# A routed two-layer network: rows of a block turned by a transposing DMA, three inner buffers, and the fp16 cast shared by two engines

## The reference

```python
x = x + linear_attention(layernorm(x), W_attn, b_attn, W_proj, b_proj)   # 16 heads of 8
z = layernorm(x)
logits = z @ Wr + br                                # 8 experts
route_w = softmax(logits); top 2, renormalised
h = relu(z @ W1[e] + b1[e])                         # 128 -> 512, for each expert e
expert_out = h @ W2[e] + b2[e]                      # 512 -> 128
x = x + sum over the two chosen e of routed[e] * expert_out[e]
```

## Time and profile before

| | |
|---|---|
| median of 3 runs | 367.26 us (367.24 to 367.77) |
| the profiled execution | 367.57 us |
| its span, first to last instruction | 365.8 us |
| TensorE busy (matmul) | 301.8 us, 83% of the span |
| VectorE busy | 306.2 us, 84% |
| ScalarE busy | 220.0 us, 60% |
| GpSimd busy | 258.0 us, 71% |
| DMA traffic | 29.25 MB, mean 80 GB/s |
| mean granted TensorE clock | 0.935 of full speed |

### The profile page before, as it was taken

The page is one execution under the profiler, slowest core; times in us unless marked ns, Lnnn a source line. Parts: engine busy times, 40 slices in busy tenths (PEclk is TensorE's granted clock), DMA queues, the critical chain, the costliest instruction groups (busy, mean ns, idle before and its releaser), DMA issues.

```text
span 365.8 us, 8190 instructions
## 1 busy us (share of the span) xinstructions
PE 301.8 (83%) x2374; PEld 223.3 (61%) x2377; DVE 306.2 (84%) x622; ACT 220.0 (60%) x644; POOL 258.0 (71%) x254
## 2 busy tenths in 40 slices
PE   5789999779979999899585877999999999998200
PEld 5578755335545445545343766789999999997100
DVE  6988899998787999998897197999888888888186
ACT  2778502387788544444247864667777777775082
POOL 3749999744979999877786663777777777666400
PEclk9999999989999999999786599999999999999755
DMA  7990000000000000011111531224333333211298
GB/s 220 352 282 9 2 0 0 0 4 0 1 0 2 0 15 25 22 37 59 53 44 45 154 82 49 71 68 139 95 88 102 96 97 103 74 43 42 80 391 253
DMA packets 23957, 29.25 MB, mean 80 GB/s; under 512 B 3806, under 2 KB 18569, under 8 KB 23916
## 3 DMA queue, kind: packets, MB, share of 16 engines
q1 hardware_dynamic: 18934, 19.02, 17.9%
q0 software_dynamic: 4544, 9.38, 7.9%
q10 hardware_dynamic: 438, 0.33, 0.3%
HBM read 16.04 MB, written 12.67 MB: 79 GB/s over the span
## 4 chain that ended last, share of the span: by engine, by line
POOL 27%; PE 21%; issue 20%; DVE 19%; ACT 9%; DMA 3%; POOLq 1%; SPq 0%; DVEq 0%; ACTq 0%
POOL y_rows L568 18%; POOL x_rows L528 8%; PE ps L1272 6%; PE ps L1271 4%; DVE nd L926 4%; DVE work L915 3%; PE ps L1245 2%; ACT qk L772 2%; DVE rows L942 2%; ACT v L657 1%; ACT xs L676 1%; DVE x L1206 1%; PE ps L1247 1%; DVE st L801 1%; PE ps L1311 1%
## 5 line engine op out<-in xcount | busy, mean ns | idle before, releaser
L568 POOL DMA_INDIRECT y_rows<-kvt,yid x78 | 74.7, 958 | 29.3 <-issue 19.5
L737 ACT ACTIVATE ps<-ps,b1s 128x256 f32<-128x256 f32 x156 | 60.1, 448 | 35.2 <-PE ps L1427 35.2
L528 POOL DMA_INDIRECT x_rows<-rows,pos_i x64 | 62.4, 975 | 24.5 <-issue 18.0
L1152 DVE CAST wraw<-ps 128x1024 f16<-128x1024 f32 x39 | 47.7, 1224 | 14.0 <-ACT ps L737 11.5
L1156 DVE TENSOR_TENSOR wraw<-ps,wraw 128x1024 f16<-128x1024 f32 x39 | 47.8, 1224 | 1.3
L1425 PE MATMUL ps<-wraw,w1h 128*128 128x256 f16 x156 | 43.4, 278 | 5.7 <-DVE wraw L1156 3.5
L1444 PE MATMUL ps<-w,wraw 128*128 x312 | 45.3, 221 | 0.0
L1445 PE MATMUL ps<-w,wraw 128*128 x312 | 44.9, 221 | 0.0
L1426 PE MATMUL ps<-wraw,w1h 128*128 128x256 f16 x156 | 43.3, 277 | 0.0
L1427 PE MATMUL ps<-wraw,w1l 128*128 128x256 f16 x156 | 43.1, 277 | 0.0
L915 DVE TENSOR_TENSOR work<-ps,qk 128x1024 f32<-128x1024 f32 x32 | 38.0, 1214 | 5.7 <-PE ps L1272 5.6
(11 more groups left out here) (242 smaller groups left out, 768.1 us busy)
## 6 DMA issues: line engine op xcount, KB each, us to landing
wraw<-x_rows SPq DMA_DIRECT2D x39, 130.0 KB
qk<-y_rows SPq DMA_DIRECT2D x8, 512.0 KB, 6.4
wraw<-in_L_ffn_W_dram SPq DMA_DIRECT2D x1, 2048.0 KB, 11.5
out_dram<-x SPq DMA_DIRECT2D x8, 256.0 KB, 4.6
x<-in_L_attn_x_dram SPq DMA_DIRECT2D x3, 512.0 KB, 7.5
y_rows<-kvt,yid POOLq DMA_INDIRECT x78, 2.2
x_rows<-empty SPq DMA_DIRECT2D x9, 130.0 KB, 3.2
x_rows<-rows,pos_i POOLq DMA_INDIRECT x64, 2.4
```

The source lines that it names most:

```text
L528: nc.gpsimd.indirect_dma_start(out=x_rows, out_offset=bass.IndirectOffsetOnAxis(ap=pos_i[:, c, t:t + 1], axis=0), in_=rows[:, t, :], in_of ...
L568: nc.gpsimd.indirect_dma_start(out=y_rows, in_=ysb[:, n % YG, g], in_offset=None, out_offset=bass.IndirectOffsetOnAxis(ap=yid[:, n, g:g + ...
L737: ins = nc.scalar.activation(o, o, ACT.Relu, bias=b1s[:, bass.ds(e * HC + c, 1)])
L1152: nc.vector.tensor_copy(hh[:, n % 2], inner(n)).then_inc(hi_done, 1)
```

## The change

Four things are done together:

- SP's load of a block becomes two. A transposing DMA reads the 256 rows of 256 fp16 numbers from `x_rows` and writes them transposed to `xgT`, which now has six buffers; a second DMA reads the two extra words of each row to `ids`. Both wait for `up_done` of the block six before, in place of `turn_done`. `turn_block` and `copy_turned` are gone, and with them `xg` and PSUM banks 0 and 1 as their place.
- `hh`, `hl` and the PSUM banks of the inner layer are three buffers (`HB`), not two. `up(n)` waits for `lo_done` of block n - 3.
- The cast to `hh` is shared: VectorE casts the first 512 columns, as soon as ScalarE has applied relu to them, and ScalarE the other 512, behind its four relus and a wait for them. `hidden_low` and `down` wait for both.
- The order of rows in a block is different (slot g * 128 + p in place of 2p + g), for `slot_i` and the numbers alike.

Its core:

```diff
+    HB = 3
...
-        hh = in_w(2 * HC * SLOTS, F16).rearrange("p (b c n) -> p b c n", b=2, c=HC)
-        hl = in_w(2 * HC * SLOTS, F16).rearrange("p (b c n) -> p b c n", b=2, c=HC)
-        xg_w = in_w(XG * GPB * ROW).rearrange("p (b n) -> p b n", b=XG)
-        xg = xg_w.rearrange("p b (g w) -> p b g w", g=GPB)
-        xgT = in_w(2 * 2 * SLOTS, F16).rearrange("p (b w n) -> p b w n", b=2, w=2)
+        hh = in_w(HB * HC * SLOTS, F16).rearrange("p (b c n) -> p b c n", b=HB, c=HC)
+        hl = in_w(HB * HC * SLOTS, F16).rearrange("p (b c n) -> p b c n", b=HB, c=HC)
+        xgT = in_w(XG * 2 * SLOTS, F16).rearrange("p (b w n) -> p b w n", b=XG, w=2)
+        ids = in_w(XG * GPB * 2).rearrange("p (b g w) -> p b g w", b=XG, g=GPB)
...
                 if n >= XG:
-                    sp.wait_ge(turn_done, n - XG + 1)
+                    sp.wait_ge(up_done, n - XG + 1)
                     sp.wait_ge(yid_done, n - XG + 1)
-                sp.dma_start(xg_w[:, b, :], x_rows[bass.ds(row, SLOTS), :].rearrange("(p g) w -> p (g w)", g=GPB)
-                             ).then_inc(loaded[b], 16)
+                rows_of_block = x_rows[bass.ds(row, SLOTS), :]
+                sp.dma_start_transpose(xgT[:, b], rows_of_block[:, 0:D].bitcast(F16)).then_inc(x_turned[b], 16)
+                sp.dma_start(ids[:, b], rows_of_block[:, D:ROW].rearrange("(g p) w -> p g w", p=P)).then_inc(ids_in[b], 16)
...
-            def copy_turned(n):
...
                 for c in range(HC):
                     at = c % 2 * SLOTS
-                    o = ps[:, 2 + 2 * (n % 2) + c // 2, at:at + SLOTS]
+                    o = ps[:, 2 * (n % HB) + c // 2, at:at + SLOTS]
                     ins = nc.scalar.activation(o, o, ACT.Relu, bias=b1s[:, bass.ds(e * HC + c, 1)])
-                ins.then_inc(hid_done, 1)
+                    if c % 2 == 1:
+                        ins.then_inc(hid_done, 1)
+                if n >= HB:
+                    act.wait_ge(down_done, n - HB + 1)
+                act.wait_ge(hid_done, 2 * n + 2)
+                nc.scalar.activation(hh[:, n % HB, 2:HC].rearrange("p c n -> p (c n)"), ps[:, 2 * (n % HB) + 1, :],
+                                     ACT.Copy).then_inc(hi2_done, 1)
...
             def hidden_high(n):
-                dve.wait_ge(hid_done, n + 1)
-                if n >= 2:
-                    dve.wait_ge(down_done, n - 1)
-                nc.vector.tensor_copy(hh[:, n % 2], inner(n)).then_inc(hi_done, 1)
+                dve.wait_ge(hid_done, 2 * n + 1)
+                if n >= HB:
+                    dve.wait_ge(down_done, n - HB + 1)
+                nc.vector.tensor_copy(hh[:, n % HB, 0:2], inner(n)[:, 0:2]).then_inc(hi_done, 1)
 
             def hidden_low(n):
                 dve.wait_ge(hi_done, n + 1)
-                nc.vector.tensor_tensor(hl[:, n % 2], inner(n), hh[:, n % 2], ALU.subtract).then_inc(lo_done, 1)
+                dve.wait_ge(hi2_done, n + 1)
+                nc.vector.tensor_tensor(hl[:, n % HB], inner(n), hh[:, n % HB], ALU.subtract).then_inc(lo_done, 1)
...
-            def turn_block(n):
...
-                pe.wait_ge(turn_out, n + 1)
-                if n >= 2:
-                    pe.wait_ge(lo_done, n - 1)
-                xh, xl = xgT[:, n % 2, 0], xgT[:, n % 2, 1]
+                pe.wait_ge(x_turned[n % XG], 16 * (n // XG + 1))
+                if n >= HB:
+                    pe.wait_ge(lo_done, n - HB + 1)
+                xh, xl = xgT[:, n % XG, 0], xgT[:, n % XG, 1]
...
                 pe.wait_ge(hi_done, n + 1)
+                pe.wait_ge(hi2_done, n + 1)
```

More of the change, by code:

```diff
@@ L323, in block_kernel @@
         table_done = sem("table_done")
-        loaded = [sem(f"loaded{b}") for b in range(XG)]
+        x_turned = [sem(f"x_turned{b}") for b in range(XG)]
+        ids_in = [sem(f"ids_in{b}") for b in range(XG)]
         yid_done = sem("yid_done")
-        turn_done = sem("turn_done")
-        turn_out = sem("turn_out")
         up_done = sem("up_done")
@@ L330, in block_kernel @@
         hi_done = sem("hi_done")
+        hi2_done = sem("hi2_done")
         lo_done = sem("lo_done")
@@ L1396, in _ @@
             regs = [pe.alloc_register(name=f"pe_expert{b}") for b in range(4)]
-            def turn_block(n):
-                pe.wait_ge(loaded[n % XG], 16 * (n // XG + 1))
-                if n >= 2:
-                    pe.wait_ge(turn_out, n - 1)
-                both = xg[:, n % XG, :, 0:D].bitcast(F16)
-                for g in range(GPB):
-                    for w in range(2):
-                        at = w * SLOTS + g * P
-                        ins = nc.tensor.matmul(ps[:, n % 2, at:at + P], both[:, g, w * D:(w + 1) * D], ident_h[:, :],
-                                               start=True, stop=True)
-                ins.then_inc(turn_done, 1)
             def up(n):
@@ L1448, in down @@
                     for c in range(HC):
-                        ins = nc.tensor.matmul(o, hl[:, n % 2, c, g * P:(g + 1) * P], high[c], start=False,
+                        ins = nc.tensor.matmul(o, hl[:, n % HB, c, g * P:(g + 1) * P], high[c], start=False,
                                                stop=(g == GPB - 1 and c == HC - 1))
@@ L1465, in _ @@
             logits(U - 1)
-            turn_block(2)
-            turn_block(3)
             for n in range(NBLK):
```

32 lines of the change are left out of this document (9 added, 23 removed).

## The result

The changed kernel takes 363.09 us (median of 4 runs, 362.47 to 364.00) against 367.25 (366.22 to 367.77) for the kernel before on the same chip: a ratio of 0.989, 95% interval 0.986 to 0.992. It is faster by 4.2 us, less than half of the 8.6 that was forecast; the time itself lies inside the stated range, near its upper end. The profiled execution took 364.0, its span 362.3; before it was 367.57 and 365.8.

What follows compares the result with a forecast made beforehand. POOL's row of scatters, started by `pos_i`, was the bound, with TensorE's pace over the last 5.3 us. `pos_i` 0.13 + 2 x 0.55 + 2.04 = 3.27 us earlier and no late waits: 8.6 off 367.57, 359.0; range 356.5 to 363.5.

Steps and rivals of the forecast that it cites:

- What bounds the kernel, `pos_i` first: POOL's scatters start when `pos_i` comes and then hardly rest; `pos_i` was to come 3.27 us earlier, at 220.5.
- Part 1: Before `pos_i`: with three inner buffers TensorE reaches the ranks earlier and VectorE's 2.04 us of idle go.
- Part 2: VectorE's cast shared with ScalarE: 0.69 us in place of 1.23, saving 0.54 to 0.55 a block.
- the handoff: TensorE through ScalarE's relus, half copy and copy of y: 2.88 us, averaged with TensorE's 2.77 to 2.83 a block.
- TensorE's lead: Last copy of y ends at 326.6 us, needed by 332.5: 6 us to spare, so TensorE leaves the end.
- Part 4: Loads on SP's queue: at most 2.6 us a block, latency hidden by a lead of six blocks or 16 us.
- rival A: Transposing DMA on SP's queue and the DMA engines sets the end above 3.2 us a block: about 403 us, 15%.
- Rival C: TensorE keeps 3.10 us a block because the path through ScalarE takes what turning gave: 361.2 us, 7%.
- B: `pos_i` gains less than 3.3 us, as the first transposed block or the clock's rise comes late: 361 us, 16%.
- D: DMA traffic stretches POOL's scatters by 0.1 us each, as much as is gained: 367 us, 3%.
- The sum: POOL's last scatter starts at 333.8, not 342.39, 8.6 us earlier, with 23.4 us behind it unchanged: 359.0 us, 55%.

Runs made afterwards that it cites:

- two banks: Changed kernel with y alternating between two PSUM banks from block 12 on: 359.81 us against 367.28 for the kernel before, ratio 0.980.

## Why the prediction fell short, point by point

- **What bounds the kernel, `pos_i` first**: right. `pos_i` ended at 220.08 (forecast 220.5), POOL took it up 0.77 later and began y at 236.00 (forecast 236.4).
- **Part 1, three inner buffers**: right, the 2.04 us went and the 2.03 stay when the buffers are two.
- **Part 2, the split cast**: the duration was right (0.69; the 1.23 that it starts from is 1.21 in the earlier trace rows, which changes nothing). That ScalarE's half copy would cost the logits nothing net was right against the kernel before (212.01 against a forecast of 212.37), but the comparison hid that with the transposing DMA alone they are copied at 210.58: against that the two half copies cost them 1.4.
- **Part 2, the handoff, (2.88 + 2.77)/2 = 2.83: the step that failed.** Its term for TensorE, 2.77, holds 1.46 for `down`, taken from the earlier trace rows, one of the fastest blocks: there the sequencer had gone through most of the register instructions under `up`. It was 1.88 in the changed kernel. The clue was in the trace of before: the 0.11 a block that the prediction called small gaps lies wholly in `down`, whose mean was 1.56 and not 1.46. Of the 0.42 that the term lacked, then, 0.10 was there before the change, about 0.16 came with the turning gone (1.72 with two banks, 1.74 with the DMA alone), and about 0.16 with the late copy of y, which the half copy put only 0.16 to 0.62 ahead of b2. The last of these was also priced wrongly as a wait: from y seen to the end of the first eight matmuls the prediction has 0.14 + 0.11 + 0.44 = 0.69, and the block shown has 1.39 (321.54 to 322.93). A loop worked out afterwards with 1.31 there gives 1.31 + 0.44 + 0.44 (rest of `down`) + 1.31 (`up`) + 0.31 + 1.54 (relus) + 0.03 + 0.49 (half copy) + 0.38 = 6.25 for two blocks, 3.13 a block; measured 3.20. With the register instructions taken away it was 2.87, and the forecast's alternation can be seen, blocks of 2.78 and 2.95 in turn.
- **TensorE's lead**: the forecast gave it 6.4 us in the stage ruled by VectorE, and block 7's copy of y did come 7.0 earlier (238.00 for 244.97). Then 29 blocks were to gain 7.8 and lost 2.8. The last copy of y ended at 336.75, not at about 326.6, and the 6 us to spare were gone.
- **Part 4, the loads, and rival A**: right that they stay hidden. SP's queue:

```profile
202.49 1.19 SPq L404 DMA_TRANSPOSE wraw<-x_rows  x1
203.87 0.43 SPq L405 DMA_DIRECT2D wraw<-x_rows  x1
204.85 1.22 SPq L404 DMA_TRANSPOSE wraw<-x_rows  x1
```

  A block takes 2.36 us of the queue, within the 2.6 taken as most and under the 3.2 at which loads would have set the end; the first `up`, at 204.11, waits for nothing though its rows were asked for at 200.00. By the Trainium skill, "VectorE: DVE Perf Modes", section The three transpose paths, four tiles one after another would be an estimated 5.2 us; this trace doesn't agree. That transposing DMAs are as fast as regular ones ("Advanced Engine Details and Errata", X-Bar Transpose (TRN2)) it neither shows nor denies: 2.36 a block here, 1.33 for a plain load in the earlier trace rows, both hidden.
- **Rival C** was the nearest: it named TensorE as the bound and the handoff through ScalarE as the cause, at 361.2 with a pace of 3.10. Its mechanism is right only in part, since what grew was `down` and not the time through ScalarE. Its own threshold held: it has TensorE take over from POOL above some 3.03 us a block, and with two banks, at 3.03, the last scatter was where POOL's row alone puts it (334.5 for 236.91 + 77 x 1.265 = 334.3). **B** and **D** did not come: a scatter is still 0.96.
- **The sum again**: 338.29 - 333.8 = 4.5 us late, and 24.0 us behind the last scatter, not 23.4; with both, 359.0 becomes 364.1, and the profiled execution took 364.0. What the other 0.6 is was not looked into.

## What to carry to other kernels

A wait placed ahead of matmuls whose addresses come from a register also holds back their register instructions (here `down` took 1.88 us with a late wait, 1.72 with an early one, 1.47 with fixed addresses): before an edit makes such a wait late, count them in the view of the line, and price them as exposed. A duration read from one block in which a sequencer was ahead is a lower bound, not the cost; take the mean over many blocks. And matmuls taken from an engine may come back as late starts of those that stay: turning was 0.22 us of TensorE a block and, alone, worth nothing.

## What the runs showed of the hardware that was not expected

- A matmul of `down` with its address from registers starts 0.12 to 0.13 us after the one before in the changed kernel when y was copied late, against 0.055 with a fixed address (each register instruction is 46 ns in the records).
- A transposing DMA of 256 rows of 512 B holds SP's queue for 1.2 us, median 1208 ns in the 39 of this kernel, and the plain load of 256 pairs 0.43.
- The first pairs, asked for at 201.54, kept VectorE waiting until 206.11, 4.6 us, twice what the first plain load of 130 KB took to land in the earlier trace rows.
- Runs of the same kernel fall into two kinds, 366 to 368 and 423 to 427 us, and a gain of 1.1% in the one was a loss of 0.5% in the other. In the second kind engines stop for up to 23 us, waiting for something that the profile doesn't name.
